# Gates spread over partitions by DMA through DRAM, probabilities divided by ScalarE, and two steps moved by a slot, in a cross-attention and expert-attention kernel

## The reference

```
# layer 1: cross-attention to 77 context rows, merged by a 512x512 matrix
x1 = x + merge(softmax(where(mask, -1e9, layernorm(x) @ ctx.T / sqrt(512))) @ ctx) + bias   # merge acts along the sequence
# layer 2: 16 experts of head size 64; the 8x512 rows are read as 8x512 (causal attention within a batch)
h  = layernorm(x1)
rw = softmax over the active experts of (normalised h @ normalised sim - sigmoid(gates))     # [rows, 16]
q  = sum_e rw[e] * (h @ q_proj[e]);  k, v likewise
attn  = softmax(causal(q @ k.T / 8)) @ v                       # [rows, 64]
mixed = attn[:, None, :] * rw[:, :, None]                      # [rows, 16, 64]
out   = x1 + sum_e mixed[:, e, :] @ o_proj[e]
```

## Time and profile before

| | before |
|---|---|
| median of 3 runs | 947.69 us |
| the profiled execution | 950.48 us |
| its span, first to last instruction | 948.8 us |
| PE, PE weight loads | 96%, 90% busy |
| DVE, ACT, POOL | 68%, 22%, 14% busy |
| DMA | 71.57 MB, 75 GB/s over the span |

### The profile page before, as it was taken

The page is one execution under the profiler, slowest core; times in us unless marked ns, Lnnn a source line. Parts: engine busy times, 40 slices in busy tenths (PEclk is TensorE's granted clock), DMA queues, the critical chain, the costliest instruction groups (busy, mean ns, idle before and its releaser), DMA issues.

```text
span 948.8 us, 16504 instructions
## 1 busy us (share of the span) xinstructions
PE 913.8 (96%) x5128; PEld 853.4 (90%) x5128; DVE 648.4 (68%) x1964; ACT 213.4 (22%) x554; POOL 133.8 (14%) x383
## 2 busy tenths in 40 slices
PE   6779999999999999999999999999999999999987
PEld 5679899999999999999999999999999999999976
DVE  6778777767586675867667576876758676665743
ACT  4522321212122121212212131211312121121111
POOL 3243111101111110111111011110101110010100
PEclk9789999999999999999999999999999999999997
DMA  8821411224120331114111141112312131010110
GB/s 270 327 59 36 154 33 38 61 65 131 48 69 26 97 103 47 58 37 148 49 48 57 39 159 35 66 39 69 130 34 69 36 112 48 36 51 31 35 45 22
DMA packets 46086, 71.57 MB, mean 75 GB/s; under 512 B 9529, under 2 KB 16089, under 8 KB 45762
## 3 DMA queue, kind: packets, MB, share of 16 engines
q1 hardware_dynamic: 46018, 70.80, 22.9%
HBM read 51.90 MB, written 18.87 MB: 75 GB/s over the span
## 4 chain that ended last, share of the span: by engine, by line
PE 77%; DVE 8%; issue 6%; DMA 5%; SPq 2%; DVEq 1%; POOLq 1%; POOL 1%; ACT 0%; ACTq 0%
PE psQ L1213 44%; PE psO L1318 10%; PE psM L1318 9%; DMA merge_lo<-merge_scratch 3%; PE psT L1131 2%; PE psO L1154 2%; PE psM L1293 2%; PE psT L1163 2%; PE psT L1261 2%; DMA MASK<-in_mask 2%; DVE acc L919 1%; PE psT L1146 1%; DVE neg_mx L1036 1%; DVE b_stats L868 1%; PE psT L1240 1%
## 5 line engine op out<-in xcount | busy, mean ns | idle before, releaser
L1213 PE MATMUL psQ<-Wqkv_hi,hT_hi 128*128 128x384 f32 (+1 forms) x1024 | 350.7, 342 | 5.0 <-DVE hT_lo L793 2.9
L1213 PE MATMUL psQ<-Wqkv_lo,hT_hi 128*128 128x384 f32 (+1 forms) x1024 | 348.8, 341 | 0.0
L1213 PE MATMUL psQ<-Wqkv_hi,hT_lo 128*128 128x384 f32 (+1 forms) x1024 | 348.1, 340 | 0.0
L919 DVE SCALAR_TENSOR_TENSOR acc<-psQ,RW,acc 128x192 f32<-128x192 f32 x448 | 164.1, 411 | 145.5 <-PE psQ L1213 144.1
L1213 PEld LDWEIGHTS psQ<-Wqkv_hi,hT_hi 128*128 128x128 f32 x1024 | 194.5, 190 | 10.9 <-DVE hT_lo L793 3.3
L1213 PEld LDWEIGHTS psQ<-Wqkv_lo,hT_hi 128*128 128x128 f32 x1024 | 194.2, 190 | 4.3
L1213 PEld LDWEIGHTS psQ<-Wqkv_hi,hT_lo 128*128 128x128 f32 x1024 | 194.2, 190 | 0.0
L504 POOL TENSOR_TENSOR pow_tmp<-b_mv,eps 128x1 f32<-128x1 f32 x32 | 7.5, 236 | 659.3 <-DVE b_mv L870 659.3
L751 ACT ACTIVATE mixedT_hi<-mixed_f 128x512 fp32r<-128x512 f32 x64 | 40.5, 632 | 241.6 <-DVE mixed_f L1088 172.3
L615 ACT ACTIVATE hT_hi<-psT 128x512 fp32r<-128x512 f32 x64 | 38.2, 597 | 142.1 <-PE psT L1131 141.6
L1318 PE MATMUL psO<-Wo_hi,mixedT_hi 128*128 128x512 f32 x128 | 53.7, 419 | 0.7 <-DVE mixedT_lo L1078 0.7
(11 more groups left out here) (187 smaller groups left out, 1331.8 us busy)
## 6 DMA issues: line engine op xcount, KB each, us to landing
X<-in_x SPq DMA_DIRECT2D x32, 256.0 KB, 2.7
x_scratch<-X SPq DMA_DIRECT2D x32, 256.0 KB, 2.0
resid<-x_scratch SPq DMA_DIRECT2D x32, 256.0 KB, 3.9
out<-resid SPq DMA_DIRECT2D x32, 256.0 KB, 2.0
merge_hi<-merge_scratch SPq DMA_DIRECT2D x28, 256.0 KB, 2.9
merge_lo<-merge_scratch SPq DMA_DIRECT2D x28, 256.0 KB, 3.4
H<-in_x SPq DMA_DIRECT2D x27, 256.0 KB, 2.8
W_raw<-in_w_qkv SPq DMA_DIRECT2D x8, 768.0 KB, 10.5
```

What stands on the lines that cost most here:

```text
L919: dve.scalar_tensor_tensor(out=acc[e][:], in0=src, scalar=w, in1=acc[e][:], op0=ALU.mult, op1=ALU.add).then_inc(expert_added, 1)
L1213: last = pe.matmul(psQ[g % 4][:, 0:first_col(g) + PW], a[:, c * P:(c + 1) * P], w[:, c, E + g * PW - first_col(g):E + (g + 1) * PW], start ...
```

## The change

The gates are no longer divided by the softmax sum. They are transposed as they come from the gating (`RW`, slots 11 and 29 of their own batch), copied once by DVE into `gatesT` (16 partitions), stored to a DRAM scratch by SP a slot later, and loaded back with each expert's row repeated on 64 partitions: two DMAs of 64 partitions by 8 rows by 1 KB, at slot 16 and at slot 3 of the next batch. The PE matmuls that spread them are gone, with the matrix that POOL built, and so is POOL's product. The division is done by ACT on the probabilities, in place, between the exponential and the transposition (`SCALE_AT`); the transpositions of the probabilities and the values matmuls each move one slot later; the reciprocal moves to the start of its slot. Mixing multiplies the loaded `spread` in SBUF in place. Of the two pairs of context transpositions of slot 23 one moves to slot 22. The tables now count on past 32: 34 is slot 2 of the next batch.

```diff
-PROBS_T_AT = {20: 0, 22: 1, 4: 2, 6: 3}
-GATES_T_AT = {24: 0, 8: 1}
-VALUES_AT = {24: 0, 8: 1}
+PROBS_T_AT = ({21: 0, 23: 1, 37: 2, 39: 3},) * 2
+SCALE_AT = ({20: 0, 22: 1, 36: 2, 38: 3},) * 2
+GATES_T_AT = {11: 0, 29: 1}
+SPREAD_SLOT = 16
+SPREAD_1_SLOT = 3
+VALUES_AT = ({25: 0, 41: 1},) * 2
...
-CENTRE_AT, CTX_T_AT = 21, 23
+CENTRE_AT, CTX_T_AT = 21, {22: (0,), 23: (2,)}
...
+                def load_spread(b, h):
+                    gate = gates_dram[bass.ds(b, 1), h].rearrange("a e l -> (a e) l")
+                    half = 2 * b + h
+                    parts = [gate[part:part + E - 1:2, :].partition_broadcast(DH) for part in range(2)]
+                    if not is_first(b) or h:
+                        sp.wait_ge(mix_lo, 4 * half)
+                    sp.wait_ge(st_gates, 16 * half + 16)
+                    for part in range(2):
+                        sp.dma_start(spread[part * DH:(part + 1) * DH, :, :], parts[part]).then_inc(spread_in, 16)
...
-                            pool.tensor_tensor(twice, rw, inv, ALU.mult).then_inc(gates_divided, 1)
...
+                            act.wait_ge(inv_made, TILES * ab + i + 1)
+                            act.activation(rows, rows, ACT.Copy, scale=p_inv[i % 2][:, 0:1]).then_inc(probs_scaled, 1)
...
-                            bank = next_bank(exp_done, TILES * ab + i + 1)
+                            bank = next_bank(probs_scaled, TILES * ab + i + 1)
...
-                                last = pe.matmul(bank[:, s * 2 * P:(s + 1) * 2 * P], spread[:, 2 * u + s, :],
-                                                 gatesT[:], start=True, stop=True)
...
-                            dve.wait_ge(moved, moves.step())
+                            dve.wait_ge(spread_in, 32 * (2 * ab + h + 1))
                             dve.wait_ge(attT_out, 2 * ab + h + 1)
...
-                            dve.tensor_tensor(mixed_f[u % 2][:], psT[moves.bank()][:].rearrange("p (c l) -> p c l", c=2),
-                                              attT[:].unsqueeze(1).broadcast_to([P, 2, 2 * P]), ALU.mult
+                            pair_of = spread[:, 2 * u:2 * u + 2, :]
+                            dve.tensor_tensor(pair_of, pair_of, attT[:].unsqueeze(1).broadcast_to([P, 2, 2 * P]), ALU.mult
```

More of the change, by code:

```diff
@@ L192, in cross_attention_then_experts_kernel @@
         attT = sb("attT", [P, 2 * P])
[L193 to L196, removed]
+        gatesT = sb("gatesT", [E, 2 * P])
+        spread = sb("spread", [P, OC, 2 * P])
         mixedT = pair("mixedT", [P, 4, 2 * P])
@@ L1000, in body @@
                             w_low(k + 4)
+                        if attn and job(INVERT_AT, k, b) is not None:
+                            i = job(INVERT_AT, k, b)
+                            a = TILES * ab + i
+                            dve.wait_ge(exp_done, a + 1)
+                            if not isinstance(b, int) or a >= 2:
+                                dve.wait_ge(probs_scaled, a - 1)
+                            dve.reciprocal(p_inv[i % 2][:], p_sum[i % 2][:]).then_inc(inv_made, 1)
                         if qkv and g == GATES_1_SLOT:
@@ L1021, in body @@
                                               ALU.subtract).then_inc(wo_lo, 1)
-                        if attn and k in Y_AT:
-                            i = Y_AT[k]
+                        if attn and job(Y_AT, k, b) is not None:
+                            i = job(Y_AT, k, b)
                             h2 = 2 * ab + i // 2
@@ L1064, in body @@
                                               ALU.subtract).then_inc(v_lo, 1)
-                        if attn and k in GATES_T_AT:
-                            h = GATES_T_AT[k]
-                            where = (slice(32, GK), slice(0, 2 * P))
-                            lo(gatesT[where], None, gatesT[where], lambda bank: bank[32:GK, 0:2 * P])
-                        if qkv and k == CTX_T_AT and live(b + 2, B):
-                            low_ctx()
+                        if qkv and k in GATES_T_AT:
+                            n = 2 * b + GATES_T_AT[k]
+                            dve.wait_ge(moved, moves.step())
+                            if not is_first(b) or GATES_T_AT[k]:
+                                dve.wait_ge(st_gates, 16 * n)
+                            dve.tensor_copy(gatesT[:], psT[moves.bank()][0:E, 0:2 * P]).then_inc(moved_lo, 1)
@@ L1132, in move_rows, with move_ctx @@
                     last.then_inc(moved, 1)
-                def move_ctx(tile, n):
-                    for c in range(0, KC, 2):
+                def move_ctx(tile, n, chunks=(0, 2)):
+                    for c in chunks:
                         bank = ctx_bank(next_bank(centred, n + 1))
@@ L1279, in body @@
                             last.then_inc(scored, 1)
-                        if attn and k in VALUES_AT:
-                            h = VALUES_AT[k]
+                        if attn and job(VALUES_AT, k, b) is not None:
+                            h = job(VALUES_AT, k, b)
                             pe.wait_ge(exp_done, TILES * ab + 2 * h + 2)
@@ L1303, in body @@
                             sum_G(q, [part[:] for part in merge])
[L1304 to L1305 removed]
+                        if attn and job(PROJECT_AT, k, b) is not None:
+                            h, u, parts = job(PROJECT_AT, k, b)
                             h2 = 2 * ab + h
```

231 lines of the change are left out of this document (98 added, 133 removed), and 3 rows, old and new, of the table MIX_AT.

## The result

| | before | after |
|---|---|---|
| median of the runs, us | 947.71 (947.27 to 949.32) | 931.43 (929.84 to 932.01) |
| profiled execution, us | 950.48 | 931.50 |
| its span, us | 948.8 | 929.8 |

The ratio is 0.9823, 95% interval 0.9806 to 0.9840. The forecast was 931.8 us. Between the two profiled executions lie 19.0 us, between the medians 16.3; the sum of the prediction had 15.9.

A forecast was written before the change was run, and what follows sets the result against it. PE's instruction stream was taken to bound the body, with the drain priced apart. Gains of 14.4 + 0.8 + 1.4 less 0.7 gave 15.9 us, hence 931.8 us; own range 928.5 to 935.5, 8 in 10 range 926.5 to 938.5.

The forecast's parts named there:

- The bound: From about 65 to 915 us PE's own stream sets the pace; whatever leaves it shortens the run one for one.
- The pairs, 14.4 us: 60 body pairs of spreading matmuls leave PE's stream at 0.24 us each: 14.4 us gained.
- The projection's rate, 0.8 us: The 30 projection blocks following a pair might gain 0.05 us each, 1.5 us; half counted, 0.8 us gained.
- MASK, 1.4 us: Probability transposes move behind slot 6's transposition, loading H and MASK 0.44 us sooner; four slot 8 waits shrink: 1.4 us gained.
- The waits for the merge matrix, no change: Between its issue at slot 21 and use at slot 23 PE does the same work, so these waits stay.
- rival 3: More goes than the pairs: the 1.9 us merge-matrix wait and its clock cost vanish too, 927 us; chance 12%.
- Division in the body, nothing: ACT's 32 divisions of probabilities, taken as 13 us, are covered by PE's expert matmuls: no cost.
- The drain, 0.7 us longer: The division delays the fourth tile's transposes by 0.9 us, less 0.24 for the last pair: about 0.7 us longer.
- rival 2: In mixing slots DVE's 0.6 us slack is eaten, PE waits for `mixedT_lo`, half the gain goes: 940 us; chance 8%.
- The spreading load, 4 us: Each half's 1.05 MB load takes 4 us, with 5 us before it meets X, resid and H: no cost.
- rival 1: Loads repeating the same rows are slow and delay H and MASK in six batches: 960 us; chance 5%.
- The base: The profiled execution stands 2.8 us above the median of 947.69; subtracting this turns 934.6 us into 931.8.

The follow-up runs named there:

- after_pairs_back: Kernel after with two 128x256 matmuls issued again in each mixing slot, 60 pairs put back, their result unread: 945.95 us.
- after_again: Kernel after, unchanged, in another profiled execution: 931.13 us.
- before_again: Kernel before, unchanged, in another profiled execution: median 947.50 us.
- before_probs7: Kernel before with the four transposes of the fourth tile's probabilities in slot 7 instead of 6: 949.00 us.
- after_load_slot5: Kernel after with the load of the second half's gates in slot 5 instead of 3, ahead of H and MASK in SP's queue: 977.02 us.
- after_loads_twice: Kernel after with each spreading load issued a second time, into a DRAM tensor that nothing reads: 961.95 us.

## Why the prediction came out right

- **The bound.** PE's stream sets the pace from 65 us to the drain, and what leaves it comes off one for one. It held: PE's busy time and the span fell by the same 19.0 us, and the pairs put back brought 14.5 us of the time back.
- **The pairs, 14.4 us.** Right. The middle batches and after_pairs_back, 14.5 us for 60 pairs, agree with 0.24 us a pair; a second pair at the same place costs 0.19 us in the mean.
- **The projection's rate, 0.8 us.** Wrong, and of the other sign. The prediction compared a block behind a pair (2.80 us) with one behind an expert product (2.75) and took that for the rule. Most blocks stand behind a transpose or a small matmul, and there they open with 0.31 us and last 2.84. Added up over PE's timeline, the 60 full blocks of the body take 169.1 us before and 169.6 after: half a microsecond lost. One pair of slots was too few to tell a rule from.
- **MASK, 1.4 us.** The size was right between the two profiled executions (1.9 to 0.7 us), with luck: other executions with the order of after wait 1.0 to 2.2 us in all, after_again 1.3, before_again 2.0, so the usual gain is nearer 0.6 us, and the 0.3 us or less that was to be seen never came with the load at slot 3. The reason was wrong. The step that failed is "H and MASK are issued when PE has done the transposition of slot 6": before_probs7 moved just that, and in the four batches with a wait H was issued as late as before. The wait that ends last on SP in these batches is the one for X, whose rows DVE must have normalised, and H stands two issues behind. What helped was a third tile's copy leaving DVE's queue ahead of the normalisation, which the prediction did not list. It read X's issue and the end of slot 6's transposes, and not H's own issue at 502.9, 0.5 us behind the end of the row of these transposes.
- **The waits for the merge matrix, no change.** 3.1 us became 1.7. It is the term that rival 3 spoke of, in part: the long one at 113 us shrank to 0.3, and the half-clock stretch behind it went. By before_again two thirds of that was chance, and after_pairs_back, which waits 1.0 us there, leaves it open whether the rest is the order's doing.
- **Division in the body, nothing.** Right: without it the slots have the same length. One of 128x512 takes 0.71 us instead of the 0.65 assumed; all 32 take 17.8 us where 13 were taken.

```profile
L713 ACT ACTIVATE probs<-probs,p_inv 128x128 f32<-128x128 f32 (+3 forms) x32 | 17.8, 557 | 28.2 <-DVE p_inv L1007 28.2
```

- **The drain, 0.7 us longer.** Right in its link: the fourth tile's transposes come 0.68 us later, counted from the last slot (12.16 against 923.79 - 912.31 = 11.48), where 0.9 was taken. From there to the end the kernel after is 0.43 us faster; how much of that is the pair was not separated. So 0.25 us remain in these two executions. Others give a drain of 35.0 to 36.0 us before and 36.2 to 37.5 after; the half-clock stretch in it lasts 6.8 to 17.1 us.
- **Mixing, rival 2.** Did not come. DVE takes 680 ns for a mixing from SBUF, as before from PSUM, and PE waits for `mixedT_lo` only in the drain.
- **The spreading load, 4 us.** Wrong by a factor of two: 8.2 us from the first issue to the last landing, where "within 6 us" was to be seen. It did not matter where it stands. By the prediction's own rule, (8.2 - 5.4) x 6, it would have cost 17 us and turned the sign; H landed 0.6 us later behind its issue in the mean of the middle batches, 1.1 us in the one shown, since a load in flight does not hold the next one back in full. So rival 1 was priced too high for slot 3, and its mechanism is real: two slots later the same load costs 45.6 us.
- **The base.** The profiled execution was 2.8 us above the median. Subtracting that, as the prediction did, was right: the medians are 16.3 us apart and the sum had 15.9. Some of the agreement is luck: the projection's rate missed by 1.3 us and MASK usually by some 0.8, and shorter merge waits and a better first batch, neither of them forecast, made up for it.

## What to carry to other kernels

Where one engine's stream sets the pace, count the instructions that leave it by the distance between starts, and look at several neighbours before a difference of some hundredths is taken for a rule. For each wait on a load, follow the issuing queue back to the wait that ends last on it: it may be another engine's, for another load that stands ahead. A large load is nearly free where its queue has room and dear two slots on, and a wait of a few microseconds costs more than itself where the clock falls with it. A wait or a clock stretch seen in one execution is to be looked for in a second one before it enters a sum.

## What the runs showed of the hardware

- 1.05 MB read as 1,024 pieces of 1 KB took 8.2 us, 128 GB/s, at one place and 7.5 to 8.4 us at the others, and as long from 512 distinct pieces a DMA as from 8 pieces read 64 times. The mean rate of the queue while busy, 326 GB/s, was no guide.
- H's 256 KB land 2.8 to 3.8 us behind their issue in the middle batches of the kernel before, 3.3 to 4.2 us with 1 MB in flight that was issued 6 to 7 us earlier, and 6.7 to 8.5 us with 1 MB issued 2 to 3 us earlier.
- During PE's waits of 5.1 to 5.8 us in after_load_slot5 a stretch with a granted clock of 0.50 began, 6.8 us long in five of six batches. Behind the 1.9 us wait of before it was 3.4 us long. Behind a wait of 1.8 us in after_loads_twice (at 100.7 us), of 1.2 us in the kernel after (at 325.1 us) and of 0.7 us in before_again there was none.
- A block of twelve 512-column matmuls takes 2.75 us behind a 384-column matmul or two pairs of 256 columns, 2.80 behind one pair, 2.84 behind 128-column transposes.
